# GpSimd clears a scratch area and drains its queue behind each gather of the score passes

## What is computed

```python
K = typed_linear(x, Wk, bk, node_type)      # 19 node types, 192 columns each
Q = typed_linear(x, Wq, bq, node_type)
V = typed_linear(x, Wv, bv, node_type)
att, v = edge_msgs(K[row], Q[col], V[row], e1, e2)      # row, col: ends of an edge
att_i, v_i = edge_msgs(K[col], Q[row], V[col], e2, e1)
att = seg_softmax(att, col, n)
att_i = seg_softmax(att_i, row, n)
agg = segment_sum([v * att, e0], col) + segment_sum([v_i * att_i, e0], row)
```

## Time and profile before

| | before |
|---|---|
| median of 3 runs | 4517.4 us (4517.17 to 4521.95) |
| profiled execution | 4514.8 us |
| its span, first to last instruction | 4513.0 us |
| granted TensorE clock, mean | 0.761 |
| busy: TensorE / VectorE / ScalarE / GpSimd | 2845.5 / 2409.3 / 1721.4 / 2876.4 us |
| score passes | about 1998 to 2706 us and 3066 to 3773 us |

### The profile page before, as it was taken

The page is one execution under the profiler, slowest core; times in us unless marked ns, Lnnn a source line. Parts: engine busy times, 40 slices in busy tenths (PEclk is TensorE's granted clock), DMA queues, the critical chain, the costliest instruction groups (busy, mean ns, idle before and its releaser), DMA issues.

```text
span 4513.0 us, 51523 instructions
## 1 busy us (share of the span) xinstructions
PE 2845.5 (63%) x13735; PEld 1923.5 (43%) x13735; DVE 2409.3 (53%) x5005; ACT 1721.4 (38%) x4345; POOL 2876.4 (64%) x2661
## 2 busy tenths in 40 slices
PE   4200005545473990767777778996777777996698
PEld 1000003333362660224444447884444445885455
DVE  6434434444451114336777775556777776665353
ACT  2222310000021112125555556774555555885451
POOL 4777776666667887665555557996555553555640
PEclk5555556777785995777777778997777778997798
DMA  5444449333345653677676676777887765664300
GB/s 163 134 136 127 141 116 245 91 93 93 89 90 191 196 183 101 212 220 215 202 212 207 203 191 163 204 193 190 208 210 208 209 203 141 173 173 131 102 1 29
DMA packets 805880, 720.83 MB, mean 160 GB/s; under 512 B 424290, under 2 KB 700364, under 8 KB 805469
## 3 DMA queue, kind: packets, MB, share of 16 engines
q1 hardware_dynamic: 645116, 399.08, 31.1%
q0 software_dynamic: 153536, 315.11, 25.1%
q10 hardware_dynamic: 6944, 3.34, 0.3%
HBM read 482.09 MB, written 241.99 MB: 160 GB/s over the span
## 4 chain that ended last, share of the span: by engine, by line
DVE 20%; POOL 16%; another core or an unknown queue 12%; PE 12%; issue 9%; ACT 7%; DVEq 4%; ACTq 2%; DMA 1%; SPq 1%; POOLq 0%
POOL rec_src L564 9%; DVE META L1423 7%; POOL AR L1661 4%; DVE BIGR L648 3%; DVE AR L1443 3%; ACT AR L1717 2%; DVEq L1439 2%; DVE AR L639 2%; DVE AR L1436 2%; ACT AR L1719 1%; ACT AR L1547 1%; PE ps L1822 1%; PE ps L2433 1%; ACTq L1718 1%
## 5 line engine op out<-in xcount | busy, mean ns | idle before, releaser
L1392 POOL DMA_INDIRECT AR<-kv_tab,META x832 | 791.0, 951 | 599.8 <-DVE AR L1436 337.0
L536 POOL DMA_INDIRECT rec_dst<-AR,slot_e x400 | 484.6, 1211 | 166.7 <-issue 166.4
L1423 DVE TENSOR_REDUCE META<-ps 128x8 f32<-128x1024 f32 x416 | 507.7, 1221 | 97.9 <-remote 57.7
L668 PE MATMUL ps<-AR 128*128 128x256 f32 x832 | 305.6, 532 | 362.4 <-issue 151.0
L622 POOL DMA_INDIRECT AR<-xn_tab,META x416 | 397.9, 956 | 199.7 <-issue 128.6
L1661 POOL TENSOR_TENSOR AR<-AR 128x896 f32<-128x896 f32 x208 | 352.1, 1693 | 233.3 <-ACT AR L1726 230.4
L1626 DVE TENSOR_TENSOR BIGR<-BIGR,ps 128x260 f32 x832 | 353.6, 425 | 228.9 <-PE ps L1700 144.6
L1700 PE MATMUL ps<-AR 128*128 128x260 f32 x1664 | 419.5, 395 | 11.3 <-POOL AR L1661 5.4
L1521 PE MATMUL ps<-AR,identb 128*128 128x512 bf16 x832 | 405.4, 487 | 15.4 <-issue 8.5
L564 POOL DMA_INDIRECT rec_src<-AR,slot_e x290 | 351.8, 1213 | 91.8 <-issue 88.3
L668 PEld LDWEIGHTS ps<-AR 128*128 128x128 f32 x832 | 212.8, 268 | 456.1 <-issue 262.3
(11 more groups left out here) (432 smaller groups left out, 5815.7 us busy)
## 6 DMA issues: line engine op xcount, KB each, us to landing
v_dst<-AR SPq DMA_DIRECT2D x104, 384.0 KB
AR<-v_dst SPq DMA_DIRECT2D x104, 384.0 KB
v_src<-AR SPq DMA_DIRECT2D x104, 384.0 KB
AR<-v_src SPq DMA_DIRECT2D x104, 384.0 KB
AR<-in_W_qvk SPq DMA_DIRECT2D x44, 608.0 KB
rec_raw<-AR SPq DMA_DIRECT2D x40, 640.0 KB, 3.3
AR<-rec_dst SPq DMA_DIRECT2D x104, 192.0 KB
AR<-rec_src SPq DMA_DIRECT2D x104, 192.0 KB
```

What stands on the lines that cost most here:

```text
L536: pool.indirect_dma_start(rec_tab[0], bass.IndirectOffsetOnAxis(ap=slot_e[0][0:EP, c * CC + k:c * CC + k + 1].bitcast(U32), axis=0), RD[s] ...
L668: ins = pe.matmul(l0_ps(s, u), OW[s][:, u, :], GA[s][:, u, :], start=True, stop=True)
L1392: pool.indirect_dma_start(KVR[s][:, u, 0:KV], None, kv_tab, bass.IndirectOffsetOnAxis(ap=META[o][:, g * U + u, 0:1].bitcast(U32), axis=0)) ...
L1423: ve.tensor_reduce(BMALL[o][:, g * U + 2 * half:g * U + 2 * half + 2, :].rearrange("p b h -> p (b h)"), PSA[:, 2048 + 1024 * half:3072 + 1 ...
```

## The change

One tile of 128 x 128 fp32 is added, and behind each of the four gathers of a group GpSimd writes zeros to 128 columns of it and drains its queue. Nothing reads the tile.

```diff
@@ -108,6 +108,7 @@
         ttype = sb("ttype", [1, TT], I32)
+        PAD = sb("PAD", [P, P])
@@ -1392,6 +1393,8 @@
                     pool.indirect_dma_start(KVR[s][:, u, 0:KV], None, kv_tab,
                                             bass.IndirectOffsetOnAxis(ap=META[o][:, g * U + u, 0:1].bitcast(U32), axis=0)
                                             ).then_inc(sem(f"rows{s}"), 16)
+                    pool.memset(PAD[:, 0:128], 0.0)
+                    pool.drain()
```

## The result

The changed kernel takes 6474.2 us, the kernel before 4517.6 us on the same chip: a ratio of 1.434 (95% interval 1.429 to 1.439), 1957 us more where 202 us had been forecast. The direction was right, the size was off by a factor of ten, and the time lies far outside the range.

The account below looks back on a forecast made before the run. The prediction took the TensorE, ScalarE and VectorE loop to bound the score passes now, and GpSimd after the change: 0.95 + 0.22 + 0.75 = 1.92 us per gather, 7.75 us per group, +204 us, 4720 us; range 4600 to 4830 us, 4960 with a slower clock.

Parts of the forecast that it names:

- What bounds the kernel before: Score passes: the loop of TensorE, ScalarE and VectorE sets 6.66 us per group, and GpSimd's gathers run ahead of it.
- the 1.57 us per group: GpSimd in the score passes: time to spare per group of four gathers, 0.39 us per gather.
- remote: VectorE's product L1436: 3.05 us idle before it, put down to TensorE's lookup L1502 as the one candidate left.
- The memset: GpSimd behind each gather: clearing 128 fp32 columns adds 0.22 us.
- the 1.36 us expected without a drain: GpSimd's gather spacing with the memset alone: 0.95 + 0.22 + 0.19 us, the lower end.
- The drain: GpSimd behind each memset: holds the queue until the memset is done, exposing 0.75 us before the next gather; spacing 1.92 us.
- The next gather's unhidden 0.70 us: GpSimd after a wait: the gather's own issue work takes 0.70 us when nothing hides it.
- The sum: Both score passes at 7.75 us per group: +101.3 and +103.1 us, together +204 us, so 4720 us.
- the landing: GpSimd's drain also waits for the gather's data: 6.0 us per gather, +3580 us, 8100 us; chance 0.02.
- The clock rival: TensorE in the score passes falls to 1.2 GHz throughout: 8.9 us per group, 237 us on top, 4957 us; chance 0.06.
- The rival by which pacing at 1.36 us removes the remote waits: VectorE's 3 us waits vanish with gathers spaced out: up to 243 us won, 4275 us; chance 0.03.
- The hidden issue work: GpSimd's next gather issue hides behind the drain: spacing 1.36 us, time stays at 4515 to 4520 us; chance 0.11.

Follow-up runs that it names:

- memset_only_2: Memset behind each gather without the drain, second run, against the kernel before: 4531.5 us against 4543.8 us, a ratio of 0.9975.
- memset_wait_2: Memset behind each gather, waited for by a semaphore in place of the drain, second run, against the kernel before: 4778.1 us against 4543.8 us.
- memset_only: Memset behind each gather without the drain, first run, against the kernel before: 4152.4 us against 4084.8 us, a ratio of 1.016.
- memset_wait: Memset behind each gather, waited for by a semaphore in place of the drain, first run, against the kernel before: 4662.9 us against 4084.8 us.
- drain_only: Drain behind each gather without the memset, against the kernel before: 6381.4 us against 4084.8 us.

## Why the prediction was wrong, step by step

1. *What bounds the kernel before:* held. Without the drain the pauses of the earlier trace rows swallow the memsets and the time does not rise (memset_only_2), so the 1.57 us per group were real there. They are not a property of the kernel alone: in the batch of 4085 us there is nothing to spare. That "remote" stands for TensorE's lookup was argued by leaving out the other candidates, though the load of the time features (semaphore "edges") had not been excluded; the semaphore records bear it out. The product of the earlier trace rows at 2145.41 starts 0.02 us behind the update of "q" at 2145.39, and the lookup that gives it, L1502, is recorded as ended at 2142.38.
2. *The memset:* 0.22 us, right, and the 1.36 us expected without a drain were 1.34.
3. *The drain:* the step that failed, in "It holds GpSimd's queue until the memset is done" and "The drain itself adds little", read from the earlier trace rows. Those rows have a drain behind a computation on its own engine. In the change it stands behind a DMA issue too, and a gather is done for it only when its data has landed: 3.15 us from the gather's start to the drain's end where I had 1.22 (0.95 + 0.22 + 0.05). That is 1.93 us per gather more. The next gather's unhidden 0.70 us, the other half of the step, is exact: 0.70 in the median of 831.
4. *The sum:* with 1.94 us per gather it comes within 30 us (memset_wait_2). With the landing in it, the spacings are 3.84, 3.84 and 3.92 us in the median and 4.34 us behind the gather that opens a group, which lands after 3.57 us and not 3.06 (why is not shown). A group takes 15.97 us in the median, 16.23 on average; 2 x 103 x (16.23 - 6.68) = 1967 us, and the profiled execution is 1960 us longer than that of the kernel before.
5. *The rivals:* the landing was among them, with 0.02, on the ground that a drain needn't know of transfers. That was an argument without a row, while the prediction itself said that no row of this trace had a drain behind a DMA. It was also priced from the wrong row: the 5.05 us of the earlier trace rows are one case, the first group of a pass with four gathers on their way; alone on GpSimd's queue a gather lands after 3.1 us. With that the rival would have said 3.1 + 0.1 + 0.7 = 3.9 us, 15.7 us per group and 6.3 to 6.4 ms. The clock rival: the granted clock did fall, to 0.61 in the score passes, and it cost nothing, since TensorE was waiting: it was busy 605 of 1689 us, and GpSimd waited 7 us in all for VectorE. The rival by which pacing at 1.36 us removes the remote waits is refuted (memset_only_2). The hidden issue work, which the Trainium skill's sequencer description (Advanced Engine Details and Errata, Sequencer and Instruction Queues) would have allowed, doesn't hide behind a drain or a waiting nop: 0.70 us in both; behind a plain memset it does, 0.17 us.

What stays open is why TensorE's release comes late, and why it does so in some batches only. In the kernel before, 96 of 192 recorded updates of "q" come over 1 us behind the recorded end of their lookup, 3.5 us in the median of these; in memset_only_2 it is 95 of 196. In memset_only, memset_wait, drain_only and the changed kernel none does: the median is 0.014 us. Matmul ends are modelled, so the delay may lie in the lookup itself or in its signal. It doesn't depend on the gathers' spacing between 1.25 and 1.34 us, and in the batches of 4.5 ms it is gone once the gathers are 1.94 us apart (memset_wait_2).

None of the variants beats the kernel before; the memset without the drain is 0.25% under it in one batch and 1.6% over it in another.

## What to carry to other kernels

A drain on GpSimd behind a DMA that GpSimd has issued costs the DMA's landing, some 3.1 us here for 197 KB, and so puts in series the gathers that had overlapped; to order two instructions of GpSimd's own, wait for the first one's semaphore instead (0.06 us, and the next gather's 0.70 us of issue work exposed). Price an instruction from a row where it stands behind the same kind of instruction; if the trace has none, a rival that rests on that gap needs a real chance, not two in a hundred. An engine's spare time read from one profile can be gone in another batch of runs of the same kernel (1.57 us per group here, and none there).

## What the runs showed of the hardware

- GpSimd's drain ends 0.07 us behind the last landing of the one gather ahead of it, and 0.20 us behind it with four on their way, which it waits for once. With nothing on its way it costs 0.12 us. SyncE's drain takes 0.13 us with a load of 192 KB on its way.
- A gather of 128 rows of 1.5 KB lands 3.08 us behind its start, one of half the bytes 2.66 us behind. An estimate from these two: twice the 0.42 us between them, 0.84 us, goes with the bytes, and the other 2.2 us don't.
- The issue work of a gather is 0.70 us behind a drain or a wait that holds the queue, and hides behind a running instruction (0.17 us left behind a memset, 0.30 us behind another gather).
- The same kernel takes 4085 us in one batch and 4511 to 4551 us in others, with a granted clock of 0.82 and 0.76. In the slower ones, where GpSimd is not the bound, half of the updates of "q" come some 3.5 us behind the recorded end of TensorE's lookup. With GpSimd as the bound the score passes take the same time in both (2016.4 us in memset_wait and memset_wait_2).
